# First cross attention of a two-layer gated network: outputs from gathered heads, row sums from ScalarE's accumulators, one engine per copy of a pair, loads in another order

## What is computed

```python
def _L0_xattn_ref(x, kv, mask, attn_bias, WQ_w, WQ_b, WK_w, WK_b, WV_w, WV_b, WO_w, WO_b):
    Q = (x @ WQ_w.T + WQ_b).reshape(b, sq, H, DK).transpose(0, 2, 1, 3)    # H = 16, DK = 16
    ...
    T = jnp.einsum('bhqd,bhkd->bhqk', Q, K) / math.sqrt(DK) + attn_bias[:, None, :, :]
    m2 = jnp.einsum('bi,bj->bij', mask.astype(T.dtype), mask.astype(T.dtype))
    T = jnp.where(m2[:, None, :, :] == 0, -1e9, T)
    out = jnp.einsum('bhqk,bhkd->bhqd', jax.nn.softmax(T, axis=-1), V)
    return out.transpose(0, 2, 1, 3).reshape(b, sq, E) @ WO_w.T + WO_b
...
x = x + jnp.tanh(g_xattn[0]) * _L0_xattn_ref(_layernorm(x), ctx_1024, mask, bias, ...)
```

## Time and profile before

| what | value |
| --- | --- |
| runs | 2439.62, 2443.82, 2447.48 us, median 2443.82 |
| profiled execution | 2440.32 us, of which the span of the trace is 2438.5 us |
| busy in the span | PE 92%, PEld (weight loads) 62%, DVE 68%, ACT 36%, POOL 4% |
| first attention | 0 to 413.55 us of the span |
| mean granted clock of TensorE | 0.969 of full speed |

### The profile page before, as it was taken

How to read it: one execution, slowest core, us unless ns; L and a number is a source line. 1 busy time by engine, 2 the same in 40 slices (tenths; PEclk the granted TensorE clock), 3 DMA queues, 4 the chain that set the end, 5 groups by cost and what they waited for, 6 DMA issues and landing times. The chain is left out here.

```text
span 2438.5 us, 46473 instructions
## 1 busy us (share of the span) xinstructions
PE 2242.1 (92%) x18440; PEld 1517.8 (62%) x18440; DVE 1655.3 (68%) x4535; ACT 878.2 (36%) x1811; POOL 108.4 (4%) x115
## 2 busy tenths in 40 slices
PE   5889996989999999998899999999879999999998
PEld 2555554434664765775455555555768888888887
DVE  4666674566656556544777777777478787878785
ACT  3877784051230330311555555545221111111110
POOL 3331401000000000000000000000000000000000
PEclk8989898899999999999999999999899999999999
DMA  5010002100000002001000000000300000000000
GB/s 161 11 36 22 22 14 79 61 1 0 1 1 1 1 1 104 1 1 46 1 1 1 1 1 1 1 1 1 139 1 1 1 9 1 1 9 0 1 9 10
DMA packets 21571, 46.01 MB, mean 19 GB/s; under 512 B 3969, under 2 KB 12290, under 8 KB 20738
## 3 DMA queue, kind: packets, MB, share of 16 engines
q1 hardware_dynamic: 21378, 43.48, 5.2%
HBM read 37.44 MB, written 2.10 MB: 16 GB/s over the span
## 5 line engine op out<-in xcount | busy, mean ns | idle before, releaser
L2002 PEld LDWEIGHTS banks<-work,big 128*128 128x128 f32 x2048 | 249.5, 194 | 9.4 <-issue 1.9
L2002 PE MATMUL banks<-work,big 128*128 128x128 f32 x2048 | 251.3, 277 | 1.7 <-ACT work L2093 1.5
L928 PE MATMUL banks<-big,work 128*128 128x256 f32 x1024 | 241.3, 379 | 0.0
L2109 ACT ACTIVATE work<-banks 128x512 f32<-128x512 f32 x128 | 76.5, 597 | 433.1 <-PE banks L2002 433.1
L854 PE MATMUL banks<-big,work 128*128 128x512 f32 x512 | 221.2, 593 | 0.0
L539 ACT ACTIVATE work<-banks,work 128x512 f32<-128x512 f32 x256 | 173.9, 685 | 122.0 <-DVE work L628 122.0
L928 PEld LDWEIGHTS banks<-big,work 128*128 128x128 f32 x1024 | 195.3, 191 | 33.6 <-issue 1.9
L1675 ACT ACTIVATE work<-work 128x512 f32<-128x512 f32 x256 | 169.4, 713 | 19.1 <-DVE work L1769 19.1
L854 PEld LDWEIGHTS banks<-big,work 128*128 128x128 f32 x512 | 97.2, 191 | 120.2 <-issue 120.0
L628 DVE TENSOR_REDUCE work<-banks 128x2 f32<-128x1024 f32 x128 | 150.6, 1218 | 15.2 <-PE banks L430 15.2
L1132 DVE CUSTOM_DVE_ANT_0 work<-banks,work 128x512 f32<-128x512 f32 (+3 forms) x128 | 57.7, 488 | 131.9 <-PE banks L870 131.4
(11 more groups left out here) (222 smaller groups left out, 3836.7 us busy)
## 6 DMA issues: line engine op xcount, KB each, us to landing
big<-in_bias SPq DMA_DIRECT2D x16, 256.0 KB, 5.9
big<-in_B_val SPq DMA_DIRECT2D x8, 512.0 KB, 6.9
big<-in_B_out SPq DMA_DIRECT2D x1, 4096.0 KB, 20.5
big<-in_D_downT SPq DMA_DIRECT2D x1, 4096.0 KB, 13.6
big<-in_D_up SPq DMA_DIRECT2D x1, 4096.0 KB, 22.9
work<-work SPq DMA_DIRECT2D x120, 32.0 KB, 2.0
wc<-in_ctxT SPq DMA_DIRECT2D x1, 2048.0 KB, 7.8
wab<-in_L_ffn_w_q SPq DMA_DIRECT2D x1, 2048.0 KB, 9.8
```

Of the source, the lines that this page charges most:

```text
L928: last = eng.matmul(XO[qt // 2][:, qt % 2 * D:(qt % 2 + 1) * D], spread[:, c % NG, qt * P:(qt + 1) * P], w_out[:, c, :], start=False, stop ...
L2002: last = eng.matmul(HP[n % 2][:, q * P:(q + 1) * P], down[:, kc * ELO + n * NJ + q, :], xnT[par][:, kc, :], start=(kc == 0), stop=(kc == K ...
```

## The change

- The normalised group is written to `onorm` (two buffers) and gathered by `compact`, 4 copies of 16x512 in SBUF by DMA, into `whole`, where the 256 features lie dense. `outputs` needs 2 products a tile in place of 4, with dense weights, and waits for the copies. The two biases become one vector `shift` that GpSimd adds to x (`shift_x`).
- The exponentials write their row sums (`accum_out`); `sums` and its job are gone, `invert` reads `rowsum`, and `inverses` and `normalise` come a step earlier; the loop has one step less.
- VectorE copies the whole second pair (`take_pair`, 128x1024); ScalarE's `take_half` is gone.
- One job a step at most, between the two `turn_probs`; `slot` names it. The outputs stand in steps 5, 6, 10 and 12.
- The first masks come earlier, `rows` has two buffers, and `fold_rows(b + 1)` stands in batch b. The context of batches 1 to 3, the output weights and the second mask are issued before the moves. The first `scores` stand ahead of the second values.

```diff
-    onorm = [big1(G, S) for _ in range(2)]
+    onorm, whole = big1(2, S), [big1(KC, S) for _ in range(2)]
...
-    rows = take(2, S)
+    rows = [take(2, S) for _ in range(2)]
...
+    def slot(n):
         b, i = divmod(n, PER)
-        more, before = b + 1 < B, 0 < b <= B
+        more = b + 1 < B
         if i % QT == 3:
-            return ("sum", (n - 7) // QT) if n >= 7 and (n - 7) // QT < B * G else None
-        if i % QT == 0:
-            return ("mult", (n - 8) // QT) if n >= 8 and (n - 8) // QT < B * G else None
-        if i in (1, 2) and b < B:
-            return ("q" if i == 1 else "k", b, 1)
+            return ("mult", (n - 7) // QT) if n >= 7 and (n - 7) // QT < B * G else None
+        if i in (0, 1) and b < B:
+            return ("q" if i == 0 else "k", b, 1)
...
+        if i in OUT_AT and 0 < b < B:
+            return ("out", b - 1, OUT_AT.index(i))
+        if more and i in (2, 13):
+            return ("k" if i == 2 else "q", b + 1, 0)
+        if more and i in (8, 9):
+            return ("x", b + 1, i - 8)
+        if more and i in (4, 14):
+            return ("v", b + 1, 0 if i == 4 else 1)
         return None
...
-                eng.wait_ge(dve_took, TOOK[("k", b - 1, 1)])
                 eng.wait_ge(fold_step, fold_at(b - 1, QT - 1))
+            if b >= 2:
+                eng.wait_ge(dve_took, TOOK[("k", b - 2, 1)])
+            if b == 1:
+                eng.wait_ge(fold_first, FOLD)
             n = ROWS * b
             eng.tensor_scalar(mm, mraw, 0.0, None, ALU.is_equal).then_inc(row_step, 1)
             eng.tensor_scalar(mzero, mcraw, 0.0, None, ALU.is_equal).then_inc(row_step, 1)
             eng.wait_ge(row_step, n + 2)
...
+                def compact(b, g):
+
+                    eng.wait_ge(dve_took, TOOK[("mult", G * b + g)])
+                    if b >= 2:
+                        eng.wait_ge(job_made, MADE[("out", b - 2, QT - 1)])
+                    for j in range(GH):
+                        r = (g % 2 * GH + j) * DK
+                        eng.dma_start(whole[b % 2][r:r + DK, g // 2, :], onorm[STRIP * j:STRIP * j + DK, g % 2, :]
+                                      ).then_inc(compacted[g], 16)
...
                 eng.dma_start(x[:, QT:, :], tokens[:, QT:, :]).then_inc(s["x_loaded"], 16)
+                eng.dma_start(ctxT[:, :, S:], context[:, :, S:]).then_inc(ctx_rest, 16)
+                eng.dma_start(wo, a["A.woT"].rearrange("(c p) n -> p c n", p=P)).then_inc(wo_loaded, 16)
+                eng.dma_start(bo, a["L0_xattn_WO_b"].rearrange("(a n) -> a n", a=1).to_broadcast([P, D])).then_inc(wo_loaded, 16)
+                load_mask(1)
                 move(kc_, ks, ("k", 0, 0), 0, 0)
                 move(qc, qs, ("q", 0, 0), 0, 0)
-                eng.wait_ge(wo_cleared, 1)
...
-                move(qc, qs, ("q", 0, 1), 0, 1)
-                move(kc_, ks, ("k", 0, 1), 0, 1)
-                eng.dma_start(ctxT[:, :, S:], context[:, :, S:]).then_inc(ctx_rest, 16)
...
-                for b in range(1, B):
-                    load_mask(b)
-                    for t in range(QT):
-                        if b == 1 and t == 0:
-                            eng.wait_ge(fold_first, FOLD)
-                        else:
-                            eng.wait_ge(fold_step, fold_at(b - 1, t))
-                        load_bias(b, t)
-                    move(kc_, ks, ("k", b, 0), b, 0)
-                    move(qc, qs, ("q", b, 0), b, 0)
+                for b in range(B):
                     move(qc, qs, ("q", b, 1), b, 1)
                     move(kc_, ks, ("k", b, 1), b, 1)
+                    if b + 1 < B:
+                        for t in range(QT):
+                            if b + t == 0:
+                                eng.wait_ge(fold_first, FOLD)
+                            else:
+                                eng.wait_ge(fold_step, fold_at(b, t))
+                            load_bias(b + 1, t)
+                    if b:
+                        compact(b - 1, G - 1)
+                    compact(b, 0)
+                    if b + 1 < B:
+                        move(kc_, ks, ("k", b + 1, 0), b + 1, 0)
+                    compact(b, 1)
+                    if b + 1 < B:
+                        move(qc, qs, ("q", b + 1, 0), b + 1, 0)
+                    if b + 2 < B:
+                        load_mask(b + 2)
+                    compact(b, 2)
+                compact(B - 1, G - 1)
...
+                def shift_x(b):
+
+                    if b == 0:
+                        eng.wait_ge(shift_step, 2)
+                        eng.wait_ge(staged, QT)
+                    else:
+                        eng.wait_ge(staged, QT + b)
+                    for t in range(QT):
+                        xt = x[:, b * QT + t, :]
+                        eng.tensor_tensor(xt, xt, shift, ALU.add).then_inc(shifted, 1)
...
+                fold_rows(eng, 1)
                 for b in range(1, B):
-                    fold_rows(eng, b)
                     stage_x(b)
+                    if b == 1:
+                        shift_x(0)
+                    shift_x(b)
                     for t in range(QT):
                         fold_bias(eng, b, t, fold_step, fold_at(b, t) - FOLD, mm, bt)
+                    if b + 1 < B:
+                        fold_rows(eng, b + 1)
 
...
 
-                    eng.wait_ge(dve_took, TOOK[("sum", g)])
+                    eng.wait_ge(rinv_ready, g + 1)
                     bank_free(eng, ("mult", g))
...
-                    for g in range(G):
-                        last = eng.matmul(bank[:, 0:D], onorm[b % 2][:, g, t * P:(t + 1) * P], wo[:, g, :],
-                                          start=(g == 0), stop=(g == G - 1))
+                    if t == 0:
+                        for g in range(G):
+                            eng.wait_ge(compacted[g], 16 * GH * (b + 1))
+                    for kc in range(KC):
+                        last = eng.matmul(bank[:, 0:D], whole[b % 2][:, kc, t * P:(t + 1) * P], wo[:, kc, :],
+                                          start=(kc == 0), stop=(kc == KC - 1))
...
-                for c in range(2):
-                    values(0, c, TB[:, c, :])
+                values(0, 0, TB[:, 0, :])
+                scores(0)
+                values(0, 1, TB[:, 1, :])
                 keys(0, 0, OB)
...
                 def spread_probs(n, j):
                     eng.wait_ge(low_ready, GH * n + j + 1)
-                    one = prob[:, n % 2, j, :]
-                    eng.activation(one, one, ACT.Exp, bias=low[:, n % 2, j:j + 1], scale=-1.0).then_inc(p_ready, 1)
+                    if n % QT == 0 and n >= 2 * QT:
+                        eng.wait_ge(rinv_ready, n // QT - 1)
+                    one, at = prob[:, n % 2, j, :], n % QT * GH + j
+                    eng.activation(one, one, ACT.Exp, bias=low[:, n % 2, j:j + 1], scale=-1.0,
+                                   accum_out=rowsum[:, n // QT % 2, at:at + 1]).then_inc(p_ready, 1)
...
                 def invert(g):
-                    eng.wait_ge(job_made, MADE[("sum", g)])
+                    eng.wait_ge(p_ready, GH * QT * (g + 1))
                     if g >= 2:
                         eng.wait_ge(dve_took, TOOK[("mult", g - 2)])
-                    eng.reciprocal(rinv[:, g % 2, :], MB[:, 0:QT * GH]).then_inc(dve_took, 1)
+                    eng.reciprocal(rinv[:, g % 2, :], rowsum[:, g % 2, :]).then_inc(rinv_ready, 1)
 
                 def normalise(g):
                     eng.wait_ge(job_made, MADE[("mult", g)])
-                    eng.tensor_tensor(onorm[g // G % 2][:, g % G, :], MB, oT, ALU.mult).then_inc(dve_took, 1)
-
-                def take_half(n):
+                    eng.wait_ge(o_taken, g + 1)
+                    if g >= 2:
+                        eng.wait_ge(compacted[(g - 2) % G], 16 * GH * ((g - 2) // G + 1))
+                    eng.tensor_tensor(onorm[:, g % 2, :], MB, oT, ALU.mult).then_inc(dve_took, 1)
...
+                def take_pair(n):
+
                     eng.wait_ge(t_made, 2 * n + 2)
                     if n >= 4 and n % 2 == 0:
                         eng.wait_ge(av_made, n - 2)
                     at = n % 2 * P
-                    eng.tensor_copy(pT[n // 2 % 2][:, 2:4, :, at + HALF:at + P],
-                                    TB[:, 1, :].rearrange("p (j k q) -> p j k q", j=2, q=HALF)).then_inc(pt_dve, 1)
+                    eng.tensor_copy(pT[n // 2 % 2][:, 2:4, :, at:at + P].rearrange("p j k (f q) -> p (j k) f q", f=2),
+                                    TB.rearrange("p f (c q) -> p c f q", q=HALF)).then_inc(pt_dve, 1)
```

More of the change, by code:

```diff
@@ L1266, in a_attention @@
+        if more and i in (2, 13):
[4 more added lines that the diff above has]
+            return ("v", b + 1, 0 if i == 4 else 1)
+        return None
     JOBS = [("kg",), ("x", 0, 0), ("x", 0, 1), ("qg",), ("v", 0, 0), ("v", 0, 1), ("k", 0, 0), ("q", 0, 0)]
-    for n in range(LAST + 5):
```

(22 more changed lines are left out.)

149 lines of the change are left out of this document (54 added, 95 removed).

## The result

| | median us | range (runs) | ratio to before, 95% |
| --- | --- | --- | --- |
| before | 2442.37 | 2437.66 to 2447.48 (7) | |
| after | 2425.06 | 2415.67 to 2428.35 (7) | 0.9932 [0.9918, 0.9946] |

The change is faster, by 17 us where I forecast 48. In the profiled execution (2428.35 us, span 2426.3) the first attention ends at 378.30, where SyncE issues the first load of the next stage, 35.5 us earlier than before (413.84). The two middle stages kept their length (1318.6 for 1319.5). The last stage, the product-key experts, whose code the change does not touch, grew from 705.1 us (1733.38 to 2438.5) to 729.4 (1696.88 to 2426.3). So -35.5 - 1.0 + 24.3 = -12.2 us of span. Against the sum (2392.1) the profiled execution is 36 us late: 24 lie in the last stage, 13 in the first, -1 between.

The account below looks back on a forecast made before the run. TensorE, 92% busy in the second batch, was taken as the engine to look at, in a step ring with ScalarE. Steps, root, clock falls and tail summed to 2392.1 us; the median's 3.5 offset gave 2396, range 2379 to 2422.

Parts of the forecast that it names:

- the sum: First attention's steps added up to end at 365.3, 48.2 us earlier; against the profiled 2440.32 us this gives 2392.1.
- the rest of the 2438.5 us span is not touched: Everything outside the first attention's four batches was taken to keep its time.
- the clock: First attention's light steps: TensorE's granted clock falls to 0.50; 5 falls, 7.7 us, bounds 0 and 16 falls (25 us).
- root: Step 4: ScalarE computes the next batch's root, making step 5's pair some 2.0 us late in each of three batches.
- clock falls at every light run: Rival: 16 falls of TensorE's clock in the first attention, 17 us more, 2413; chance 0.15.
- The rival that the clock stays up: Fuller slots or the skill's long-wait rule prevent clock falls; the 7.7 us go, 2388; chance 0.12.
- Light steps 4.64 and job steps 5.27 us: First attention's loop: 4.64 us without a job; about 5.27 with a 2 us job between the two transposes.
- VectorE's copy: The 128x1024 copy of the second pair takes 1.22 us with 0.7 us of cover: zero cost, bounds 0 to 0.35 a step.
- gather: The last normalised group's DMA copies in the closing output add 4.0 us that nothing covers.
- tail: From the last scores to the first attention's end: 24.5 us, now 25.1.
- no wait for context or rows: TensorE's context wait (11.07 us) and VectorE's waits for mask rows (34.9 us in three) go; both costed at nothing.
- The slower rival, the stretched copy: VectorE's large copy stretched to 3 us beside GpSimd in most steps: 70 us, 2466; chance 0.04.

Follow-up runs that it names:

- e1: The change with 144 padding instructions (waits on a reached semaphore) at the start of TensorE's program: 2407.63 us, ratio 0.9869.
- e3: The kernel before with 96 padding instructions at the start of TensorE's program: 2466.75 us, ratio 1.0109.
- e4: The kernel before with 48 padding instructions at the start of TensorE's program: 2470.63 us in a single execution.
- e9: The change, unpadded, with discarded TensorE products in ten jobless steps, four before step 5's job in three batches, eight behind the last weighing: 2381.62 us, ratio 0.9749.
- e12: The change, padded at the second stage, with one discarded 128x256 product in each of ten steps without a job: 2389.4 us, ratio 0.9789.
- e7: The change padded as in e5, second pair's copy again in halves on VectorE and ScalarE, row sums still from accumulators: 2407.2 us, ratio 0.9877.
- e8: The change padded as in e5, with a single buffer for the mask's rows: 2403.29 us, ratio 0.9866.
- e10: The change padded as in e5, mask loads back in their old place on SyncE's queue, two row buffers kept: 2437.05 us, ratio 0.9977.
- e5: The change with 144 padding instructions on TensorE at the start of the second stage: 2404.69 us, ratio 0.9864.
- e2: The change with 48 padding instructions at the start of TensorE's program: 2431.77 us, ratio 0.9967.

## Why the prediction was wrong

**The step that failed: "the rest of the 2438.5 us span is not touched".** I took unchanged code for unchanged time. The last stage took 729.4 us for 705.1, 24.3 more, since the shorter program ahead moved TensorE's loop there. e1, e3 and e4 show both ways that the loop's place decides; that it is a packet's edge is worked out from the count and the packets of q8. Both halves of it could be had ahead of the result: the trace of before has a hardware loop whose rounds bring no instructions, and the two programs differ by 416 instructions of TensorE ahead of it.

**The term that was mis-sized: the clock.** Forecast 5 falls of 1.54 us, 7.7 in all. By the sum's own steps after shows 8.1 us more than forecast in the start and first batch (110.3 for 102.2), 0.0 in the second, 2.8 in the third, 10.8 in the last to its scores (81.7 for 70.9): 21.7 for 7.7. Of the 14 us difference about 1 is the start (step 3 at 38.34 for 38.0, and e9 without falls ends batch 0 at 103.1). The number of falls was about right, six stretches, five at steps without a job that the prediction named (3, 12, 50, 56, 62) and one at the root of the third batch (37). Their cost was not: against the same steps in e9 they lost 2.8, 4.6, 2.8, 6.8, 1.2 and 2.8 us, 21.0 in all, for 1.54 each. The low clock went on through steps with a job (5, 13, 51, 58), which the sum had at full speed; what sets the length of a stretch these runs do not show. The rival "clock falls at every light run" came near this size (25 us) with another picture, more and shorter falls. The rival that the clock stays up, after the Trainium skill (TensorE: Matmul & The Clock Gate, "Loop structure matters more than you think"), is refuted: near 318 us the clock fell where TensorE had not stood idle for more than 1.21 us at a time since the last root, 100 us before, and with 0.5 us of products in that idle time (e12) it did not fall in such steps.

**What held.** Light steps 4.64 and job steps 5.27 us; middle batches 80.01 (80.0); root 2.1 (2.0); VectorE's copy 1224 ns (1.22) without a cost that e7 could tell; the accumulator's read 256 times (190 ns each, the next exponential 0.09 behind its start); gather 4.68 (4.0); tail 23.2 (24.5, and 21.1 at full clock); no wait for context or rows. For the rows I named the two buffers and the earlier mask together; e8 and e10 show that only the mask's place counts. The slower rival, the stretched copy, did not occur. With the loop put back (e1, e5) the time is 2405 to 2408, inside the range and 9 to 12 above the forecast; with the clock kept too it is 2382.

## What to carry to other kernels

Before costing untouched code at nothing, look at hardware loops behind the change: count an engine's instructions ahead of the loop, and see whether instruction packets arrive within its rounds; if none do, an edit ahead can change that, and padding in a place where the engine idles longer than the padding lasts can put it back. Where steps repeat with a microsecond of idle TensorE, a product whose result is thrown away can be worth more than what it costs; here ten to 40 of them brought 12 to 20 us (e12 and e9 against e5, less the 3 us of padding that e5 shows). And of several loads moved at once, the one that ends the last wait is the one that pays: test them apart.

## What the runs showed of the hardware

- A loop of 1,672 TensorE instructions ran without fetching in the ten kernels where it lies in 7 packets of 16 KB by the count, and where it lies in 8 it fetched 9 packets in every round, with one wait of 3.2 to 3.7 us (after, e3, e4) or two of together 4.2 to 5.7 (e2). The Trainium skill (Runtime: NRT & Kernel Launch, "Instruction fetch mechanics") gives TensorE 2,048 instructions, which is 8 packets, and adds that only two lines are held and that a taken branch outside them stalls. Taken as what a loop may span, neither fits these runs: 7 packets stay, 8 do not.
- Waits on a reached semaphore are not free: 106 ns for an instruction of two, from the first products at 10.2, 15.4 and 20.4 us with 48, 96 and 144 of them. Where TensorE idled 13.4 us anyway, 104 (e12) showed nothing and 144 (e5) showed 3.2 us.
- A wait of some 3.4 us of TensorE for instructions also lowered its granted clock to 0.50 behind it; the products there took 1.4 to 2.9 us more than at the full clock.
